# Layer 0 of the second pass as three products of half the columns, with its inputs moved ahead on ScalarE

## The reference

```python
s = style @ mw.T + mb
weight = SCALE * w * s[:, None, :, None]
weight = weight * rsqrt(sum(weight * weight, axis=(2, 3)) + EPS)[:, :, None, None]
# types of the four layers: same, upsample (then blur), same, blur then downsample
```

## Time and profile before

| | |
|---|---|
| median of the runs | 1338.16 us (1337.69 to 1339.97, 3 runs) |
| span of the profiled execution | 1336.1 us |
| TensorE busy | 1293.9 us, 97% |
| VectorE busy | 1044.7 us, 78% |
| ScalarE busy | 798.9 us, 60% |
| GpSimd busy | 806.3 us, 60% |
| from 1000 to 1200 us: TensorE, VectorE, ScalarE, GpSimd | 200.00, 157.89, 102.20, 107.61 us of 200 |

### The profile page before, as it was taken

The page is one execution under the profiler, slowest core; times in us unless marked ns, Lnnn a source line. Parts: engine busy times, 40 slices in busy tenths (PEclk is TensorE's granted clock), DMA queues, the critical chain, the costliest instruction groups (busy, mean ns, idle before and its releaser), DMA issues.

```text
span 1336.1 us, 22883 instructions
## 1 busy us (share of the span) xinstructions
PE 1293.9 (97%) x8127; PEld 1226.3 (92%) x8127; DVE 1044.7 (78%) x2442; ACT 798.9 (60%) x1625; POOL 806.3 (60%) x611
## 2 busy tenths in 40 slices
PE   3789999999999999999999999999999999999998
PEld 3589899899899999899999999999999999999998
DVE  7878878778877778778778888787878878787873
ACT  4587787778777787775445544545554554545440
POOL 6468887666676677664555545555555555555542
PEclk9899999999999999999999999999999999999999
DMA  3234444444455654452542523425243342524322
GB/s 129 77 105 134 133 133 133 133 132 133 132 140 148 155 150 141 126 160 79 119 117 85 147 77 103 130 77 151 81 123 109 95 136 78 151 80 120 111 84 88
DMA packets 86274, 158.20 MB, mean 118 GB/s; under 512 B 26633, under 2 KB 48402, under 8 KB 86034
## 3 DMA queue, kind: packets, MB, share of 16 engines
q1 hardware_dynamic: 84898, 154.79, 41.5%
q10 hardware_dynamic: 1264, 1.96, 0.5%
HBM read 93.79 MB, written 33.56 MB: 95 GB/s over the span
## 4 chain that ended last, share of the span: by engine, by line
PE 86%; DVE 5%; POOL 4%; ACT 2%; issue 1%; DMA 1%; SPq 0%; DVEq 0%; POOLq 0%; ACTq 0%
PE psum L1770 28%; PE psum L1772 27%; PE psum L1771 27%; PE psum L1884 2%; POOL xs_l L931 1%; DVE psum L1544 1%; DMA w3T<-in_w_dram 1%; POOL vs_l L926 0%; POOL vbuf L910 0%; POOL vbuf L906 0%; PE psum L283 0%; DVE y_l L1490 0%; POOL vbuf L908 0%; DVE a_l L1520 0%; DVE a_f L1525 0%
## 5 line engine op out<-in xcount | busy, mean ns | idle before, releaser
L1770 PE MATMUL psum<-wt_h,u_h 128*128 128x386 f32 (+1 forms) x760 | 260.9, 343 | 0.0
L1772 PE MATMUL psum<-wt_h,u_l 128*128 128x386 f32 (+1 forms) x760 | 257.9, 339 | 0.0
L1771 PE MATMUL psum<-wt_l,u_h 128*128 128x386 f32 (+1 forms) x760 | 257.6, 339 | 0.0
L1544 DVE STREAM_TRANSPOSE psum<-vbuf 32x256 f32<-32x256 f32 x480 | 218.8, 456 | 11.8 <-ACT vbuf L1137 0.7
L1520 DVE SCALAR_TENSOR_TENSOR a_l<-psum,tabs,a_h 128x512 fp32r<-128x512 f32 x128 | 95.9, 751 | 158.7 <-ACT a_h L1119 158.6
L906 POOL TENSOR_TENSOR vbuf<-vbuf 128x512 f32<-128x512 f32 x64 | 97.1, 1518 | 190.7 <-ACT vbuf L1151 190.7
L920 POOL TENSOR_TENSOR vm_f<-vm_f 128x512 f32<-128x512 f32 x64 | 82.7, 1292 | 177.5 <-DVE vm_l L1514 177.1
L1144 ACT ACTIVATE vbuf<-psum,tabs 128x512 f32<-128x512 f32 x128 | 105.2, 822 | 117.4 <-PE psum L1772 113.5
L1770 PE MATMUL psum<-a_h,vm_h 128*128 128x256 f32 x512 | 148.2, 289 | 3.2 <-ACT vbuf L1144 3.0
L1771 PE MATMUL psum<-a_l,vm_h 128*128 128x256 f32 x512 | 145.7, 285 | 0.0
L1770 PEld LDWEIGHTS psum<-wt_h,u_h 128*128 128x128 f32 x760 | 143.5, 189 | 2.2
(11 more groups left out here) (309 smaller groups left out, 3803.7 us busy)
## 6 DMA issues: line engine op xcount, KB each, us to landing
vm_f<-vv SPq DMA_DIRECT2D x256, 112.0 KB, 4.5
xin<-in_x_ph_dram SPq DMA_DIRECT2D x32, 512.0 KB, 5.0
xr<-in_x_row_dram SPq DMA_DIRECT2D x32, 512.0 KB, 4.2
x1d<-xr SPq DMA_DIRECT2D x64, 256.0 KB, 3.3
xin<-x1d SPq DMA_DIRECT2D x32, 512.0 KB, 5.4
xr<-x1d SPq DMA_DIRECT2D x64, 256.0 KB, 5.9
xo<-in_b_base_dram SPq DMA_DIRECT2D x32, 512.0 KB, 5.9
out_dram<-xo SPq DMA_DIRECT2D x31, 512.0 KB, 2.9
```

The source lines that it names most:

```text
L1544: ins = V.transpose(ps_x[to, :, :].rearrange("p b (k n) -> p b k n", n=P)[:, :, :, frm], v3[frm, :, :].rearrange("p b (k n) -> p b k n", n ...
L1770: nc.tensor.matmul(to, stat_h, mov_h, start=first_ and n == 0, stop=False, skip_group_check=True)
L1771: nc.tensor.matmul(to, stat_h, mov_l, start=False, stop=False, skip_group_check=True)
L1772: ins = nc.tensor.matmul(to, stat_l, mov_h, start=False, stop=end, skip_group_check=True)
```

## The change

From pair 35 on (`HALVED`) layer 0 is computed otherwise. Write M0 and M1 for the matrices of the two column parities and z for the even, o for the odd columns of the input. Both halves of the result contain (M0 + M1) z; what remains of one is M0 times a difference of neighbouring columns, and of the other M1 times (odd minus even). So there is one product of the sum matrix `ms` with z (256 columns of each batch, 512 together), evacuated as `shared`, and two products of 256 columns for each batch with the differences. VectorE adds `shared` to them in PSUM (`y_sum`). ScalarE and VectorE make `a_h`, `a_l` and `a_f` from that sum.

The inputs are prepared otherwise too: ScalarE scales xin and copies its even columns (`z_h`) directly behind layer 0 of the turn, ahead of `row_ends`; GpSimd makes two differences and `z_l` between `combined` and `xo`, and the low parts `d_l` behind `xo`, instead of one `xs_l` at the turn's end. The Toeplitz buffers of the first pass now share memory with the buffers of the second.

```diff
+HALVED = TILES + 3
+SUM_TURN = 20
...
@@ GpSimd
+            def matrices_summed():
+
+                G.tensor_tensor(ms_f[:, :], m0f[:, 1, 0, :], m0f[:, 1, 1, :], ALU.add).then_inc(ms_sum, 1)
...
+            def input_differences(g):
+
+                odd, even = xin[:, :, 1:H:2], xin[:, :, 0:H:2]
+                pool.wait_ge(in_scaled, at(g))
+                G.tensor_tensor(dif[:, :, 1:Q], xin[:, :, 1:H - 1:2], xin[:, :, 2:H:2], ALU.subtract).then_inc(dif_set, 1)
+                pool.wait_ge(dif_set, nth(g, 2, 0))
+                G.tensor_tensor(odd, odd, even, ALU.subtract).then_inc(dif_set, 1)
+                pool.wait_ge(z_hi, nth(g))
+                G.tensor_tensor(z_l[:, :, :], even, z_h[:, :, :].bitcast(F32), ALU.subtract)
+
+            def differences_low(g):
+                pool.wait_ge(in_hi, at(g))
+                G.tensor_tensor(d_l[:, :, 0, :], dif[:, :, :], d_h[:, :, 0, :].bitcast(F32), ALU.subtract)
+                G.tensor_tensor(d_l[:, :, 1, :], xin[:, :, 1:H:2], d_h[:, :, 1, :].bitcast(F32), ALU.subtract).then_inc(in_lo, 1)
...
                 if here(i):
                     combined(i)
+                if halved(i + 2):
+                    input_differences(i + 2)
...
+                if halved(i + 2):
+                    differences_low(i + 2)
...
-                    if here(i + 2):
+                    if here(i + 2) and not halved(i + 2):
                         inputs(i + 2)
@@ ScalarE
+            def even_inputs(g):
+                act.wait_ge(in_scaled, at(g))
+                A(z_h[:, :, :], xin[:, :, 0:H:2], ACT.Copy).then_inc(z_hi, 1)
+                A(dif[:, :, 0:1], xin[:, :, 0:1], ACT.Copy, scale=-1.0).then_inc(dif_begin, 1)
+
+            def differences_high(g):
+                act.wait_ge(dif_begin, nth(g))
+                act.wait_ge(dif_set, nth(g, 2, 1))
+                A(d_h[:, :, 0, :], dif[:, :, :], ACT.Copy)
+                A(d_h[:, :, 1, :], xin[:, :, 1:H:2], ACT.Copy).then_inc(in_hi, 1)
+
+            def shared_evacuated(g):
+                c, t = place(g)
+                act.wait_ge(shared_done, nth(g))
+                for b in range(2):
+                    A(shared[:, b, :], ps_pair[:, Q * b:Q * b + Q], ACT.Copy, scale=tab(c, t, b, T_S1)).then_inc(shared_out, 1)
+
+            def layer0_halved(g):
+                c, t = place(g)
+                shared_evacuated(g)
+                for b in range(2):
+                    act.wait_ge(y_sum, nth(g, 2, b))
...
+                    A(a_f[:, b, 0:1], sh.apad_h[:, c, batch(t, b), 1].bitcast(F32), ACT.Identity,
+                      bias=sh.apad_l[:, c, batch(t, b), 1].bitcast(F32))
+                    A(a_f[:, b, 1:Q], ps_x[:, b, 1:Q], ACT.Copy).then_inc(a_odd, 1)
+                    A(by_parity(a_h, b), ps_x[:, b, :].rearrange("p (r m) -> p r m", r=2), ACT.Copy).then_inc(a_hi, 1)
...
                 if here(i + 1):
                     layer0(i + 1)
+                if halved(i + 2):
+                    inputs(i + 2)
+                    even_inputs(i + 2)
                 if by_blocks(i):
                     row_ends(i)
                 if here(i + 1):
                     composed2(i + 1)
+                if halved(i + 2):
+                    differences_high(i + 2)
...
@@ VectorE
+            def layer0_halved(g):
+                c, t = place(g)
+                for b in range(2):
+                    ve.wait_ge(l0_done, at(g, 2, b))
+                    ve.wait_ge(shared_out, nth(g, 2, b))
+                    y = ps_x[:, b, :].rearrange("p (r m) -> p r m", r=2)
+                    V.scalar_tensor_tensor(out=y, in0=y, scalar=tabs[:, c, T_S1, batch(t, b)],
+                                           in1=shared[:, b, :].unsqueeze(1).to_broadcast([P, 2, Q]),
+                                           op0=ALU.mult, op1=ALU.add).then_inc(y_sum, 1)
+                for b in range(2):
+                    ve.wait_ge(a_hi, at(g, 2, b))
+                    V.tensor_tensor(by_parity(a_l, b), ps_x[:, b, :].rearrange("p (r m) -> p r m", r=2),
+                                    by_parity(a_h, b).bitcast(F32), ALU.subtract).then_inc(a_lo, 1)
+                ve.wait_ge(a_odd, at(g, 2, 1))
+                V.tensor_tensor(a_f[:, :, :], ps_x[:, :, Q:H], a_f[:, :, :], ALU.add).then_inc(as_sum, 1)
@@ TensorE
+            def layer0_halved(g):
+
+                pe.wait_ge(in_lo, at(g))
+                if g == HALVED:
+                    pe.wait_ge(ms_lo, 1)
+                pe.wait_ge(pair_out, at(g - 1, 2, 1))
+                product(ps_pair, [(ms_h[:, :], ms_l[:, :], z_h[:, :, :].rearrange("p b m -> p (b m)"),
+                                   z_l[:, :, :].rearrange("p b m -> p (b m)"))], True, True).then_inc(shared_done, 1)
+                for b in range(2):
+                    for r in range(2):
+                        ins = product(ps_x[:, b, Q * r:Q * r + Q],
+                                      [(m0_h[:, 1, r, :], m0_l[:, 1, r, :], d_h[:, b, r, :], d_l[:, b, r, :])], True, True)
+                    ins.then_inc(l0_done, 1)
...
+                    if halved(i + 1):
+                        pe.wait_ge(shared_out, nth(i + 1, 2, 1))
                     nc.tensor.transpose(ps_hwT, hw[:, :], ident[:, :]).then_inc(pe_hwT, 1)
```

More of the change, by code:

```diff
@@ L174, in build @@
         sh.vec = sb("vec", [P, 2, 2, NL])
[L176 to L181, removed]
+        with ExitStack() as first_pass:
+            lag = sb("lag", [P, 2, 3, H], FR, first_pass)
+            sh.toep_h, sh.toep_l = lag[:, 0, :, :], lag[:, 1, :, :]
+            sh.tail_h = sb("tail_h", [P, 2, 2, P], FR, first_pass)
+            sh.tail_l = sb("tail_l", [P, 2, 2, P], FR, first_pass)
+        sh.bt_h, sh.bt_l = sb("bt_h", [P, L], FR)[:, :], sb("bt_l", [P, L], FR)[:, :]
+        sh.shared = sb("shared", [P, 2, Q])
+        sh.z_h, sh.z_l = sb("z_h", [P, 2, Q], FR), sb("z_l", [P, 2, Q], FR)
+        sh.dif = sb("dif", [P, 2, Q])
         sh.iota8 = sb("iota8", [P, E])
@@ L409, in program @@
     bt_h, bt_l, toep_h, toep_l = sh.bt_h, sh.bt_l, sh.toep_h, sh.toep_l
+    shared, z_h, z_l, dif = sh.shared, sh.z_h, sh.z_l, sh.dif
     xin, x1d = sh.xin, sh.x1d
@@ L416, in program, with differences @@
     xs_l = sb("xs_l", [P, 2, H + 2], FR)
+    def differences(t):
+        return t[:, :, :].rearrange("p b n -> p (b n)")[:, 0:4 * Q].rearrange("p (b r m) -> p b r m", b=2, r=2)
+    d_h, d_l = differences(xs_h), differences(xs_l)
     a_h = sb("a_h", [P, 2, APW], FR)
@@ L523, in program @@
     wt_l = sb("wt_l", [P, KT * WCOLS], FR)
+    ms_f = sb("ms_f", [P, P])
+    ms_h, ms_l = sb("ms_h", [P, P], FR), sb("ms_l", [P, P], FR)
     ssm_in, roots_in, roles_in, late_in = sem("ssm_in"), sem("roots_in"), sem("roles_in"), sem("late_in")
@@ L561, in program @@
     in_scaled = sem("in_scaled")
+    ms_sum, ms_hi, ms_lo = sem("ms_sum"), sem("ms_hi"), sem("ms_lo")
+    z_hi, dif_set, dif_begin = sem("z_hi"), sem("dif_set"), sem("dif_begin")
+    shared_done, shared_out, y_sum = sem("shared_done"), sem("shared_out"), sem("y_sum")
     u_hi, u_lo = sem("u_hi"), sem("u_lo")
@@ L669, in by_blocks, with halved, nth @@
         return here(g) and TILES < g < LAST
+    def halved(g):
+        return here(g) and g >= HALVED
+    def nth(g, n=1, i=0):
+        return n * (g - HALVED) + i + 1
     def first(g):
@@ L931, in inputs, with matrices_low @@
                 G.tensor_tensor(xs_l[:, :, 1:H + 1], xin[:, :, :], xs_h[:, :, 1:H + 1].bitcast(F32), ALU.subtract).then_inc(in_lo, 1)
+            def matrices_summed():
+                G.tensor_tensor(ms_f[:, :], m0f[:, 1, 0, :], m0f[:, 1, 1, :], ALU.add).then_inc(ms_sum, 1)
+            def matrices_low():
+                pool.wait_ge(ms_hi, 1)
+                G.tensor_tensor(ms_l[:, :], ms_f[:, :], ms_h[:, :].bitcast(F32), ALU.subtract).then_inc(ms_lo, 1)
+            def input_differences(g):
[10 more added lines that the diff above has]
+                G.tensor_tensor(d_l[:, :, 1, :], xin[:, :, 1:H:2], d_h[:, :, 1, :].bitcast(F32), ALU.subtract).then_inc(in_lo, 1)
             def column_sums_low(g):
@@ L974, in body @@
                     r_low(1)
+                if turn_is(i, SUM_TURN):
+                    matrices_summed()
+                if turn_is(i, SUM_TURN + 2):
+                    matrices_low()
+                if halved(i + 2):
+                    differences_low(i + 2)
                 if turn_is(i, -1):
@@ L1105, in inputs_high @@
                 A(xs_h[:, :, 1:H + 1], xin[:, :, :], ACT.Copy).then_inc(in_hi, 1)
+            def even_inputs(g):
[17 more added lines that the diff above has]
+                    act.wait_ge(y_sum, nth(g, 2, b))
+                    if b == 0:
+                        act.wait_ge(as_lo, at(g - 1))
+                    if b == 0 and group(g) is not None:
+                        act.wait_ge(sh.apad_ready, group(g) + 1)
+                    A(a_f[:, b, 0:1], sh.apad_h[:, c, batch(t, b), 1].bitcast(F32), ACT.Identity,
```

(14 more changed lines are left out.)

## The result

The changed kernel takes 1413.83 us (median of 4 runs, 1410.8 to 1420.17) against 1338.76 us: a ratio of 1.0561, 95% interval 1.0535 to 1.0588. The forecast was 1407, with a range of 1356 to 1436.

A forecast was written before the change was run, and what follows sets the result against it. TensorE was taken to set the pace before, with VectorE's path 0.2 us from binding. Span 1336.1 us, +68.7 (mostly 28 turns x 2.4 = 67.2), +2.0 for the median of runs, gave 1406.8; range 1356 to 1436.

The forecast's parts named there:

- TensorE's saving: Layer 0 on TensorE takes 2.14 us instead of 2.79; 29 x 0.65 = 18.9 us saved if nothing else moves.
- The late row: VectorE's first transpose waits for ScalarE's later row_ends: starts 9.9 us after the turn's second pair product, +1.1.
- The waits for GpSimd: In VectorE's gate, instructions with two SBUF operands wait for GpSimd's steps: hw ends at 19.1 instead of 17.5 us.
- From hw to the next turn: From hw's end through the LoRA products to the next turn's second pair product: 6.7 us.
- rival (b): TensorE's clock falls to half behind the 2.7 us stops: 22 us on top if every second turn, 1429; chance 0.20.
- my case: Late row plus waits for GpSimd: turn 25.8 us, 2.4 over the old; 1387 to 1429 us, chance 0.52.
- Busy times: ScalarE busier by about 2 us and GpSimd by about 4 us a turn.
- (a): VectorE slips through gaps in GpSimd's work, no contention; late row_ends alone costs 23 us, time 1361; chance 0.18.
- (c): ScalarE's order does not delay VectorE; row starts by 8.57, all 0.65 us a turn kept, time 1319; chance 0.07.
- (d): A draw: VectorE's row starts near 9.1 without contention, time within 0.2% (2.7 us); chance 0.03.

The follow-up runs named there:

- before_ahead: Kernel before, with ScalarE's inputs and inputs_high moved directly behind layer 0, ahead of row_ends, from pair 35 on; layer 0 unchanged: 1350.2 us, ratio 1.0086.
- low_late: Changed kernel with GpSimd's two d_l subtractions moved behind pair_sums, so behind the gate: 1350.7 us, ratio 1.0086 to the kernel before.
- ends_low: Changed kernel with row_ends between inputs and even_inputs, and the two d_l subtractions behind pair_sums: 1338.1 us, ratio 0.9991 to the kernel before.
- gate_scalar: Changed kernel with the gate's difference and its product with the reciprocal as TENSOR_SCALAR with a pointer scalar: 1388.3 us, ratio 1.0375 to the kernel before.
- ends_between: Changed kernel with ScalarE's row_ends moved between inputs and even_inputs: 1387.6 us, ratio 1.0375 to the kernel before.
- filled: Changed kernel with 14 unread matmuls of 256 columns ahead of TensorE's wait for hw in each halved turn: 1394.3 us, ratio 1.0416 to the kernel before.
- ends_low_lora: As ends_low, plus VectorE's vm_l behind the LoRA factors' split and one d_l half made once hw is done: 1334.2 us, ratio 0.9962 to the kernel before.

## Why the prediction was right

**TensorE's saving.** Forecast 2.14 us for layer 0, measured 2.12. It paid nothing, as forecast, since VectorE's path had too little room: 0.3 us rather than the forecast 0.2. before_ahead (hw 0.72 later, turn 0.41 longer) and low_late (0.69 and 0.37) both give that.

**The late row.** Forecast 9.9, measured 9.52: lateness 0.7 instead of 1.1. y_sum was priced right (1.42 us for two against 0.75 each) and began at 4.57, forecast 4.6; that the two copies of `shared` took 0.83 us, not 1.03, moved nothing. The mis-sized term is ScalarE's three copies of each half, which began at 5.37 (forecast 5.4) and took 2.0 us instead of 2.4: a_h 0.59 to 0.61 instead of 0.68, a_f 0.36 to 0.38 instead of 0.46. They ended at t = 7.37 instead of 7.8. Worth alone: low_late minus ends_low, 12.6 us, 0.44 us a turn.

**The waits for GpSimd.** Forecast 1.6 us a turn, measured 1.24 (hw at 18.31 in the changed kernel, 17.07 in low_late). The chain was the forecast one, except that its third member got through: the first two waits ended with the two steps of d_l, one step ahead of my schedule, because dif and the odd columns took 1.04 us, not 1.3. For short strided steps the prediction had still put hw at 19.1. That was worked out wrongly: from its own start at 9.1, GpSimd's steps end by 17.8 then, nothing of GpSimd's stands beside the third instruction, and hw comes at 18.9. Most of the rest down to 18.31 is that GpSimd's steps began at t = 8.66 and not at 9.1, behind the shorter copies. TensorE's stop came out at 1.85 us, forecast 2.7. The Trainium skill's rule ("SBUF — State Buffer", Who interferes with whom) is borne out in both its kinds: two-operand instructions in the changed kernel, an eight-column CAST (0.84 us in gate_scalar instead of 0.17) and TENSOR_SCALARs of 8 columns (0.83 us in gate_scalar and 1.34 in ends_between instead of 0.28). TENSOR_SCALARs of one column did not wait. The rows of before showed only the first kind. The sum left the second out, which in the changed kernel's ordinary turn made no difference; in its turns with edge work (extra steps for the edges of the rows, from about 690 to 860 us) it did, as shown below under the sum.

**From hw to the next turn.** Forecast 6.7 us. Measured 6.70 (18.31 to 25.01), and the same in ends_between, low_late, filled, gate_scalar and ends_low (6.70 to 6.71), in turns in which the clock does not fall. This part of the sum was exact. ends_low_lora, which changes its first half, needs 6.53.

**The clock.** In the forecast this was rival (b), 22 us on top with a chance of 0.20. It came true beside my case: 17 stretches in the second pass, each costing 1.36 us where the turn is ordinary otherwise. filled, which removes all but one, is 19.5 us faster. So the mechanism of the forecast was right, and that its number was near was luck, two errors that cancel: the turn without a fall was 0.8 us shorter than forecast (28 x 0.8 = 22 us), and the clock, which my case left out, put 20 us back. The turns with edge work added the rest.

**The sum.** In whole times: clock 19.5 us (changed minus filled); late row 12.6 us (low_late minus ends_low); the rest, 1394.3 - 1350.7 = 43.6 us, belongs to the waits for GpSimd. Of it 28 x (25.05 - 23.77) = 36 us is in the ordinary turns. Of the remaining 8 us about 5 lie in the six turns with edge work (161.5 us together in filled against 148.8 in low_late, less 6 x 1.28), part of that being the one fall of the clock that filled kept. In the changed kernel these six last 26.4 to 29.9 us, in the kernel before 23.4 to 25.1. Its trace shows what waits in the first of them. GpSimd copies edge data between xo and d_l:

```profile
708.82 1.34 POOL L253 COPY xe<-xg 64x96 f32<-64x96 f32 x4
710.24 1.26 POOL L979 TENSOR_TENSOR xs_l<-dif,xs_h 128x512 fp32r<-128x512 f32 x1
711.46 1.29 POOL L980 TENSOR_TENSOR xs_l<-xin,xs_h 128x512 fp32r<-128x512 f32 x1
```

so the two steps meet the gate's later instructions, a TENSOR_SCALAR of eight columns (0.28 to 0.29 us alone) and the sum of the one-hot rows (0.17):

```profile
710.22 1.30 DVE L1716 TENSOR_SCALAR wexp<-iota,topf,gate 128x8 f32<-128x8 f32 x1
711.56 1.21 DVE L1719 TENSOR_TENSOR wexp<-wexp 128x8 f32<-128x8 f32 x1
```

hw ends at t = 19.13 there. The second kind of wait, which the sum left out, thus had its price in such turns of the changed kernel itself.

**Busy times.** GpSimd was busier by 108.0 us, 3.9 a turn (forecast about 4); ScalarE by 27.4 us, 1.0 a turn (forecast about 2).

Rivals (a), (c) and (d) are out: the waits exist, and neither a gain nor a draw came about. What (c) named as its condition, a row at 8.57, no run reached. The nearest is 8.81 to 8.82, as before the change: in ends_between the turn is 24.83 with it, while GpSimd stands beside the gate, and in ends_low 23.33.

## What to carry to other kernels

Before you save work on the engine that bounds a kernel, measure how late the others may be: here 0.65 us a turn was saved on an engine whose next supplier had 0.3 us. Look at what two engines do at the same moment and not only at how busy each is: here two GpSimd steps of 1.3 us beside VectorE's chain of 0.16 us instructions cost 1.24 us a turn (hw at 18.31 against 17.07), and the same two steps later in GpSimd's queue cost nothing there. A regular short stop of TensorE can cost twice, once as waiting and once as a lower clock: filling it gave 19.5 us back here.

## What was not expected of the hardware

How often the clock fell changed with very small changes of a periodic stop. In the changed kernel TensorE is idle for 1.85 us ahead of hwT in 20 of the 28 turns; in 10 of these 20 the clock fell behind it, in 10 it did not. In ends_between and gate_scalar, with hw earlier by 0.19 and 0.18 us and the stop shorter by as much, it fell in 2 and 3 stretches of the whole second pass, all in the six turns with edge work. In low_late, ends_low and ends_low_lora, with 0.6 us and less in ordinary turns, it fell in none before the last microseconds of the kernel.

The length of one stop alone does not decide it. Single stops of 2.09 us in low_late and of 3.10 us in ends_between passed without a fall, while one of 3.11 us in gate_scalar, in the same turn of the loop, had one. The turns' length changed together with the stop in these kernels, and no run separates the two; what decides stays open.

ScalarE's copy of 512 columns from PSUM to a_h takes 0.59 to 0.61 us in the changed kernel and 0.68 before. Two things changed with it, and no run separates them: it reads PSUM in one run instead of with a step of two, and it no longer multiplies by the scale T_S1.
